# Reordering Pool's work in a mixture-of-experts stage: row adds behind an expert's own loads, earlier gathers, gate products first

## The chip, the cores and the metric

The kernel runs on all 8 NeuronCores of one Trainium2 chip. Each core computes one batch element, and no core talks to another. The metric is the device time of the slowest core, in microseconds (us). Five engines work side by side on a core: TensorE (PE, matrix products), VectorE (DVE), ScalarE (ACT), GpSimd (POOL) and SyncE (SP). They wait for one another through semaphores. Data moves through 16 DMA engines. In this kernel everything that Pool issues (converting weight loads, indirect gathers, indirect adds) goes through one queue, called q0 in the profile; what SP issues goes through q1.

## The reference, cut to what matters

```python
# per batch element: x is (2048, 1024)
x = x + attention(layernorm(x))            # Q = K = V = layernorm(x) @ Wq + bq, one head
n = layernorm(x)
scores = sigmoid(n @ gate_w.T)             # 32 experts
_, ids = top_k(scores + e_bias, 4)         # 4 experts for each token
w = scores[ids] / sum(scores[ids])
g = einsum('th,ehi->tei', n, w1)           # H = 1024, I = 768
u = einsum('th,ehi->tei', n, w3)
a = silu(g) * u * combine                  # combine: w for the 4 chosen experts, 0 else
x = x + einsum('tei,eih->th', a, w2)
```

Each token uses 4 of 32 experts, so a core has 8192 pairs of token and expert, 256 for an expert in the mean. The kernel computes an expert only for the tokens that chose it.

## The kernel before, in words

**First stage.** Attention, the second layer norm and the routing run first. Normalized tokens are written to device memory as bf16 (`xnd`), `out` receives the attention result, and the routing writes for each expert a list of its tokens with their weights. `t_meta` holds these lists: for each expert three blocks of 128 places (`NB = 3`), each place a row number and a weight. Places that no token takes point to spare rows behind the 2048 real ones. `t_cnt` holds the number of tokens for each expert. Weights of the first experts are loaded during this stage.

**Weights.** An expert has three weight units: `w1`, `w3` and `w2`, numbered `3*ei`, `3*ei+1`, `3*ei+2`. A unit is 128 partitions of 6144 values. `load_unit` reads it as f32 from device memory and the DMA converts it to bf16: 768 pieces with 2 KB on the destination side, issued by Pool. 16 of the 96 units (`CONV`: 7 to 10, then 17, 24, ... 94) were converted to device memory during the first stage and come through SP's queue instead. On chip there are 11 places (`RING`), so unit `u` can be loaded once unit `u-11` has been used: the places of expert `ei` receive w2 of expert `ei+3` and then w1 and w3 of expert `ei+4`.

**One expert**, on TensorE in this order:

- `gu(ei)`: for each of 6 column blocks a gate product (w1) and an up product (w3), each 8 matmuls of 128x384, into four PSUM banks of `pss`: banks 0 and 1 for gates, 2 and 3 for ups, by turns. ScalarE takes SiLU of a gate bank into `sil` (two places), VectorE multiplies with the up bank into `at`.
- `tx(ei+1)`: 24 transposes of the gathered rows `xg` of the next expert, copied by ScalarE into `xgt`. It waits for that expert's gather.
- `w2(ei)`: for three blocks and two halves, 6 matmuls of 128x512 into one of two banks of `pav`. VectorE and ScalarE evict them, scaled by the routing weight, into `yb`. `yb` has 6 buffers, which is two experts, so these evictions wait until the row adds of expert `ei-2` have landed (`y_sc.get(ei - 2)`).

`gather(ei)` is three indirect DMAs, 128 rows each, into `xg` (two experts deep; it waits for `tx(ei-2)`). `scatter(ei)` is three indirect DMAs that add rows of `yb` to `out` in device memory; it waits until the adds of expert `ei-1` have landed, because two experts can add to the same row. Blocks 0 and 1 always add 128 rows, the last block 32, 64, 96 or 128, picked by branches on the count.

**Pool's order** is the order of these calls. For one expert it is: load the places of w1 and w3 after all of `gu(ei)`; `scatter(ei-1)`; `gather(ei+2)`; load the place of w2 after `w2(ei)`. Pool works through its list in order, so one instruction that waits holds up all behind it.

## Time and profile before

| what | value |
|---|---|
| median of 3 runs | 1649.07 us (1647.56 to 1649.4) |
| profiled execution, its own time | 1663.17 us |
| span of its slowest core (core 1) | 1661.7 us |
| spans of the 8 cores | 1633.3 to 1661.7 us |
| TensorE, busy share of the span | 75% |
| ScalarE, VectorE, Pool, busy share | 26%, 24%, 24% |
| q0 packets over the whole span, share of 16 DMA engines | 98816, 85.2% |

All views are of core 1 in one profiled execution. "Busy" counts an engine's instructions. Pool's instructions that issue DMAs are spans of issuing, not of the transfer. A DMA queue's share is the time that its packets took, over 16 engines and the stretch; two queues can overlap on an engine, so shares can add up to more than 100%. The first stage ends near 502 us, the expert stage runs from there to the end.

### The profile page before, as it was taken

The numbers are of one execution on the slowest core, as the hardware profiler recorded it, in microseconds if no ns is written. First come the engines' busy times: TensorE is split into PE (matmuls) and PEld (weight loads), VectorE is DVE, ScalarE is ACT, GpSimd is POOL, SyncE is SP. The second block draws the span as 40 slices with busy tenths as digits, with TensorE's granted clock in tenths as the row PEclk, the third lists the DMA queues.
The fourth block names the chain that finished last, engine by engine and source line by source line (L and its number), as shares of the span: only waits on it lengthen the run. The fifth ranks groups of instructions, "written<-read, shape, count | busy, mean of one in ns | idle before, by whom it ended". The sixth has DMA issues, their size and how long they took to land.

```text
span 1661.7 us, 20590 instructions; the slowest of 8 cores (1633.3 to 1661.7 us)
## 1 busy us (share of the span) xinstructions
PE 1248.2 (75%) x7210; PEld 706.6 (43%) x7210; DVE 396.6 (24%) x864; ACT 434.9 (26%) x623; POOL 405.4 (24%) x375
## 2 busy tenths in 40 slices
PE   3989999988736958666969586769696668596696
PEld 1544555554423534333535343434353334353353
DVE  3634444444341211111111111111121111121121
ACT  2743333333212212111312121212121122132131
POOL 0000202112442222232322222323222223232222
PEclk8989989888767979788979798889798798798798
DMA  7999999999642999999999999999999999999933
GB/s 166 219 191 231 239 184 230 212 222 211 140 178 44 167 192 178 189 166 188 168 180 168 190 167 182 173 182 162 188 166 187 182 183 173 187 163 176 175 68 58
DMA packets 112392, 291.80 MB, mean 176 GB/s; under 512 B 11703, under 2 KB 12087, under 8 KB 107936
## 3 DMA queue, kind: packets, MB, share of 16 engines
q0 software_dynamic: 98816, 234.86, 85.2%
q1 hardware_dynamic: 13328, 55.58, 10.5%
q8 instruction: 59, 0.97, 0.2%
q14 instruction: 45, 0.37, 0.1%
q10 hardware_dynamic: 144, 0.03, 0.0%
HBM read 374.37 MB, written 77.63 MB: 272 GB/s over the span
## 4 chain that ended last, share of the span: by engine, by line
PE 40%; DMA 38%; issue 7%; POOL 5%; ACT 4%; DVE 4%; another core or an unknown queue 1%; POOLq 0%; DVEq 0%; ACTq 0%; SPq 0%
DMA xg<-xnd,t_meta 24%; PE pss L834 13%; DMA out<-yb,t_meta 12%; PE pav L865 8%; PE pav L518 7%; PE pss L478 4%; POOL out L889 3%; PE ptr L569 3%; PE ptr L350 3%; PE pss L397 2%; POOL xg L803 1%; DMA wq<-wqd 1%; ACT xn L593 1%; ACT xgt L821 1%
## 5 line engine op out<-in xcount | busy, mean ns | idle before, releaser
L834 PE MATMUL pss<-xgt,wp 128*128 128x384 bf16 x2016 | 338.9, 328 | 1.4 <-ACT xgt L821 1.4
L350 PE MATMUL ptr<-c_idb,xg 128*128 128x128 bf16 x768 | 75.5, 270 | 307.0 <-DMA xg<-xnd,t_meta 288.6
L834 PEld LDWEIGHTS pss<-xgt,wp 128*128 128x128 bf16 x2016 | 197.9, 98 | 135.7 <-issue 4.4
L889 POOL DMA_INDIRECT out<-yb,t_meta x96 | 146.7, 1529 | 279.2 <-DMA out<-yb,t_meta 184.1
L848 DVE TENSOR_TENSOR at<-sil,pss 128x384 bf16<-128x384 bf16 x192 | 106.4, 554 | 449.0 <-PE pss L834 447.0
L350 PEld LDWEIGHTS ptr<-c_idb,xg 128*128 128x128 bf16 x768 | 62.9, 122 | 323.7 <-issue 323.3
L874 DVE TENSOR_SCALAR yb<-pav,t_meta 128x512 f32<-128x512 f32 x96 | 72.0, 750 | 526.2 <-PE pav L865 502.9
L821 ACT COPY xgt<-ptr 128x1024 bf16<-128x1024 bf16 x96 | 97.2, 1012 | 350.9 <-PE ptr L350 321.5
L845 ACT ACTIVATE sil<-pss 128x384 bf16<-128x384 f32 x192 | 94.3, 491 | 358.1 <-PE pss L834 358.1
L834 PE MATMUL pss<-xgt,wr 128*128 128x384 bf16 x1056 | 178.8, 326 | 0.0
L865 PE MATMUL pav<-wp,at 128*128 128x512 bf16 x756 | 178.4, 397 | 0.3 <-DVE yb L874 0.2
L834 PEld LDWEIGHTS pss<-xgt,wr 128*128 128x128 bf16 x1056 | 103.3, 98 | 69.4
L518 PE MATMUL pav<-vq,pt 128*128 128x512 bf16 x512 | 126.5, 410 | 0.0
L478 PE MATMUL pss<-qt 128*128 128x512 bf16 x512 | 120.8, 391 | 0.7 <-ACT c_srep L454 0.4
L865 PEld LDWEIGHTS pav<-wp,at 128*128 128x128 bf16 x756 | 75.2, 102 | 94.8 <-issue 26.6
L877 ACT ACTIVATE yb<-pav,t_meta 128x512 f32<-128x512 f32 x96 | 66.0, 687 | 189.0 <-PE pav L865 185.8
L803 POOL DMA_INDIRECT xg<-xnd,t_meta x96 | 100.1, 1043 | 30.0 <-issue 29.2
L865 PE MATMUL pav<-wr,at 128*128 128x512 bf16 x396 | 95.9, 404 | 1.0 <-DVE at L848 1.0
L518 PEld LDWEIGHTS pav<-vq,pt 128*128 128x128 bf16 x512 | 54.5, 108 | 66.9 <-issue 17.8
L252 POOL DMA_DIRECT2D wp<-w2d x22 | 18.7, 848 | 257.3 <-PE pss L834 189.8
L478 PEld LDWEIGHTS pss<-qt 128*128 128x128 bf16 x512 | 50.7, 100 | 58.0 <-issue 7.6
L569 PE MATMUL ptr<-c_gw,x2t 128*128 128x32 f32 x256 | 49.6, 369 | 33.9 <-ACT x2t L551 33.9
(98 smaller groups left out, 839.1 us busy)
## 6 DMA issues: line engine op xcount, KB each, us to landing
wp<-w3d POOLq DMA_DIRECT2D x26, 1536.0 KB, 26.9
wp<-w1d POOLq DMA_DIRECT2D x23, 1536.0 KB, 30.9
wp<-w2d POOLq DMA_DIRECT2D x22, 1536.0 KB, 31.8
wcd<-wp POOLq DMA_DIRECT2D x16, 1536.0 KB, 24.9
xb<-xd SPq DMA_DIRECT2D x32, 512.0 KB
wr<-w2d POOLq DMA_DIRECT2D x10, 1536.0 KB, 26.0
wr<-w1d POOLq DMA_DIRECT2D x9, 1536.0 KB, 36.1
wr<-wcd SPq DMA_DIRECT2D x8, 1536.0 KB, 13.6
```

The lines of the kernel that those rows point to most:

```text
L350: ins = e.transpose(dst[:, k * 128:(k + 1) * 128], src_of(k), ident)
L478: ins = e.matmul(pss[:, q * 512:(q + 1) * 512], qt[:, c * T + j * 128:c * T + (j + 1) * 128], qt[:, c * T + q * 512:c * T + (q + 1) * 512] ...
L518: ins = e.matmul(pav[:, hh * 512:(hh + 1) * 512], pt[:, (j % 2) * T + c * 128:(j % 2) * T + (c + 1) * 128], vq[:, c * H + hh * 512:c * H + ...
L569: ins = e.matmul(ptr[:, b * 512 + i * E:b * 512 + (i + 1) * E], x2t[:, o:o + 128], c_gw[:, c * E:(c + 1) * E], start=(c == 0), stop=(c == ...
L803: ga_tok[ei] = p.d(lambda e, o=o, c=c: e.indirect_dma_start(out=xg[:, o:o + H], out_offset=None, in_=xnd[:, :], in_offset=bass.IndirectOff ...
L821: tr_tok[k] = txe_tok[ei] = p.s(lambda e, b=b, dst=dst: e.copy(dstv[:, :, b * 128:(b + 1) * 128], dst.rearrange("p (c t) -> p c t", c=NH)) ...
L834: ins = e.matmul(pss[:, bnk * 512:bnk * 512 + CAP], unit_ap(u, c * ID + ic * 128, 128), xgt[:, xo + c * CAP:xo + (c + 1) * CAP], start=(c ...
L845: sl_tok[n] = p.s(lambda e, so=so, gb=gb: e.activation(sil[:, so:so + CAP], pss[:, gb * 512:gb * 512 + CAP], AF.Silu), tg, a_tok.get(n - 2))
L848: a_tok[n] = p.v(lambda e, so=so, ub=ub, ic=ic: e.tensor_tensor(at[:, ao + ic * CAP:ao + (ic + 1) * CAP], sil[:, so:so + CAP], pss[:, ub * ...
L865: ins = e.matmul(pav[:, hh * 512:(hh + 1) * 512], at[:, ao + ic * CAP + b * 128:ao + ic * CAP + (b + 1) * 128], unit_ap(3 * ei + 2, ic * H ...
L874: ybank[0] = p.v(lambda e, dst=dst, src=src, wcol=wcol: e.tensor_scalar(dst, src, wcol, None, ALU.mult), w2_tok[ei], t_ml, y_sc.get(ei - 2))
L889: return e.indirect_dma_start(out=outd[:, :], out_offset=bass.IndirectOffsetOnAxis(ap=t_meta[0:n, 2 * c:2 * c + 1], axis=0), in_=yb[0:n, y ...
```

## The change

Three things change, all in the expert stage.

1. **Order on Pool.** `gather(2)` is issued before the loop. For each expert the order becomes: load the place of w1 (now after the gate products only), load the place of w3 (after the up products), `gather(ei+3)`, load the place of w2, `scatter(ei)`. A gather is issued as soon as `tx(ei+1)` has freed its buffer.
2. **Rows added.** Block 0 still adds 128 rows. Blocks 1 and 2 both pick 16, 32, ... 128 rows by a tree of branches on the count (three compares deep, eight leaves).
3. **Order on TensorE.** `gu` computes all six gate products, then all six up products. `sil` grows from two to six places, and the four banks of `pss` are used by turns over both.

```diff
@@ -166,7 +166,7 @@
         xg = sb("xg", 2 * NB * H, BF16)
         xgt = sb("xgt", 2 * NH * CAP, BF16)
         at = sb("at", 2 * NI * CAP, BF16)
-        sil = sb("sil", 2 * CAP, BF16)
+        sil = sb("sil", NI * CAP, BF16)
         yb = sb("yb", 6 * H, F32)
 
         pss = st.enter_context(nc.psum_tensor("pss", [128, 2048], F32))
@@ -780,6 +780,7 @@
             out=t_meta[:, :].rearrange("q (b n) -> q b n", b=NB), in_=mtv),
             "dML", p.cnt("dSC"), t_mi)
 
+        g_tok = {}
         gu_tok = {}
         w2_tok = {}
         tx_tok = {}
@@ -826,30 +827,34 @@
         def gu(ei):
             xo = (ei % 2) * NH * CAP
             ao = (ei % 2) * NI * CAP
+
+            def mm(e, u, bnk, ic):
+                for c in range(NH):
+                    ins = e.matmul(pss[:, bnk * 512:bnk * 512 + CAP],
+                                   unit_ap(u, c * ID + ic * 128, 128),
+                                   xgt[:, xo + c * CAP:xo + (c + 1) * CAP],
+                                   start=(c == 0), stop=(c == NH - 1))
+                return ins
+
             for ic in range(NI):
-                gb, ub = ic % 2, 2 + ic % 2
-
-                def mm(e, u, bnk, ic=ic):
-                    for c in range(NH):
-                        ins = e.matmul(pss[:, bnk * 512:bnk * 512 + CAP],
-                                       unit_ap(u, c * ID + ic * 128, 128),
-                                       xgt[:, xo + c * CAP:xo + (c + 1) * CAP],
-                                       start=(c == 0), stop=(c == NH - 1))
-                    return ins
-                tg = p.t(lambda e, mm=mm, gb=gb: mm(e, 3 * ei, gb),
+                n = ei * NI + ic
+                gb = ic % 4
+                tg = p.t(lambda e, gb=gb, ic=ic: mm(e, 3 * ei, gb, ic),
                          txe_tok[ei], u_tok[3 * ei], *bank[gb])
-                tu = p.t(lambda e, mm=mm, ub=ub: mm(e, 3 * ei + 1, ub),
+                sl_tok[n] = p.s(lambda e, gb=gb, ic=ic: e.activation(
+                    sil[:, ic * CAP:(ic + 1) * CAP], pss[:, gb * 512:gb * 512 + CAP], AF.Silu),
+                    tg, a_tok.get(n - NI))
+                bank[gb] = (sl_tok[n],)
+            g_tok[ei] = tg
+            for ic in range(NI):
+                n = ei * NI + ic
+                ub = (NI + ic) % 4
+                tu = p.t(lambda e, ub=ub, ic=ic: mm(e, 3 * ei + 1, ub, ic),
                          u_tok[3 * ei + 1], *bank[ub])
-                n = ei * NI + ic
-                so = (n % 2) * CAP
-                sl_tok[n] = p.s(lambda e, so=so, gb=gb: e.activation(
-                    sil[:, so:so + CAP], pss[:, gb * 512:gb * 512 + CAP], AF.Silu),
-                    tg, a_tok.get(n - 2))
-                a_tok[n] = p.v(lambda e, so=so, ub=ub, ic=ic: e.tensor_tensor(
-                    at[:, ao + ic * CAP:ao + (ic + 1) * CAP], sil[:, so:so + CAP],
+                a_tok[n] = p.v(lambda e, ub=ub, ic=ic: e.tensor_tensor(
+                    at[:, ao + ic * CAP:ao + (ic + 1) * CAP], sil[:, ic * CAP:(ic + 1) * CAP],
                     pss[:, ub * 512:ub * 512 + CAP], ALU.mult),
                     tu, sl_tok[n], w2_tok.get(ei - 2))
-                bank[gb] = (sl_tok[n],)
                 bank[ub] = (a_tok[n],)
             gu_tok[ei] = tu
 
@@ -893,26 +898,26 @@
                         in_=yb[0:n, yo:yo + H], in_offset=None,
                         bounds_check=bound(e, TROWS - 1), oob_is_err=True, compute_op=ALU.add)
 
-                def add_last_rows(e, done, b=b, add_rows=add_rows):
-
+                def add_counted_rows(e, done, b=b, add_rows=add_rows):
+
+                    def pick(lo, hi):
+                        if lo == hi:
+                            done(add_rows(e, lo))
+                            return
+                        mid = (lo + hi) // 32 * 16
+                        with e.If_lt(cnt_reg, b * 128 + mid + 1):
+                            pick(lo, mid)
+                        with e.Else():
+                            pick(mid + 16, hi)
                     e.reg_load(cnt_reg, t_cnt[0:1, ei:ei + 1])
-                    with e.If_lt(cnt_reg, b * 128 + 33):
-                        done(add_rows(e, 32))
-                    with e.Else():
-                        with e.If_lt(cnt_reg, b * 128 + 65):
-                            done(add_rows(e, 64))
-                        with e.Else():
-                            with e.If_lt(cnt_reg, b * 128 + 97):
-                                done(add_rows(e, 96))
-                            with e.Else():
-                                done(add_rows(e, 128))
+                    pick(16, 128)
 
                 waits = [*ye_tok[(ei, b)], *prev]
-                if b < NB - 1:
+                if b == 0:
                     y_sc[ei] = p.d(lambda e, add_rows=add_rows: add_rows(e, 128), "dY", *waits,
                                    eng="gpsimd")
                 else:
-                    y_sc[ei] = p.put("gpsimd", add_last_rows, [*waits, v_cnt], "dY", 16,
+                    y_sc[ei] = p.put("gpsimd", add_counted_rows, [*waits, v_cnt], "dY", 16,
                                      branches=True)
 
         gather(0)
@@ -920,22 +925,19 @@
         tx(0)
         for eng in Prog.ENGINES:
             p.put(eng, lambda e: e.reg_load(ovf_reg[e.engine], t_flag[0:1, 0:1]), [v_ovf])
+        gather(2)
         for ei in range(E):
             gu(ei)
             tx(ei + 1)
             w2(ei)
 
             us = [u for u in range(RING, 3 * E) if (u - RING) // 3 == ei]
-            for u in us:
-                if (u - RING) % 3 < 2:
-                    load_unit(u, gu_tok[ei])
-            if ei >= 1:
-                scatter(ei - 1)
-            gather(ei + 2)
-            for u in us:
-                if (u - RING) % 3 == 2:
-                    load_unit(u, w2_tok[ei])
-        scatter(E - 1)
+            for u, tok in zip(us, (g_tok[ei], gu_tok[ei])):
+                load_unit(u, tok)
+            gather(ei + 3)
+            for u in us[2:]:
+                load_unit(u, w2_tok[ei])
+            scatter(ei)
         p.put("gpsimd", None, [p.cnt("dY")])
 
         ovf = nc.alloc_registers("ovf")
```

## Rows read from the trace of the kernel before

**Rows 1.** Cores: span and mean granted TensorE clock of the slowest.
```profile
core 1: 1661.7 us, clock 0.868
```

**Rows 2.** Waits, 515 to 1561 us: waiter <- awaited: us in total, times, longest.
```profile
PE ptr L350 <- DMA xg<-xnd,t_meta: 257.5, 26, 19.9
POOL wp L252 <- PE pss L834: 233.1, 16, 14.9
POOL wr L252 <- PE pss L834: 184.7, 11, 21.1
POOL out L889 <- DMA out<-yb,t_meta: 184.1, 15, 15.8
```

**Rows 3.** Busy time by stretch; last three: granted clock, DMA share, GB/s.
```profile
514.00:526.00 12.00, 11.17 (x54) 6.05 (x55) 1.65 (x3) 3.33 (x5) 0.00 (x0) 0.75 0.00 0
526.00:535.00 9.00, 8.20 (x65) 5.28 (x64) 1.68 (x4) 2.71 (x5) 1.37 (x2) 1.00 0.01 2
535.00:1561.00 1026.00, 737.42 (x4351) 416.97 (x4348) 156.16 (x252) 224.02 (x335) 274.37 (x238) 0.87 1.05 177
1561.00:1662.00 101.00, 85.55 (x504) 47.38 (x504) 18.97 (x30) 26.20 (x39) 28.16 (x21) 0.92 0.43 79
```

**Rows 4.** DMA queues, 535 to 1561 us: packets, MB, share of 16 engines.
```profile
q0 software_dynamic: 72966, 162.25, 99.2%
q1 hardware_dynamic: 1728, 18.88, 5.8%
q8 instruction: 36, 0.59, 0.2%
```

**Rows 5.** DMA, 1053 to 1062 us, only weights and few gather packets.
```profile
q0 software_dynamic: 761, 1.53, 104.5%
```

**Rows 6.** DMA, 1064 to 1069 us, almost only row adds.
```profile
DMA packets 285, 0.97 MB, mean 194 GB/s; under 512 B 34, under 2 KB 34, under 8 KB 285
...
q0 software_dynamic: 285, 0.97, 102.5%
```

**Rows 7.** DMA, 1597 to 1608 us, the row adds of expert 29 alone.
```profile
DMA packets 337, 1.20 MB, mean 109 GB/s; under 512 B 48, under 2 KB 48, under 8 KB 336
...
q0 software_dynamic: 336, 1.18, 63.4%
```

**Rows 8.** DMA, 502 to 514 us, the gathers of experts 0 and 1.
```profile
q0 software_dynamic: 480, 1.15, 34.4%
```

**Rows 9.** Pool in order of time, first experts: start, us, what [idle before].
```profile
533.63 0.89 POOL L252 DMA_DIRECT2D wp<-w2d  x1 [22.67 <-PE ptr L350]
...
535.67 1.07 POOL L803 DMA_INDIRECT xg<-xnd,t_meta  x1 [0.27 <-issue]
...
559.32 0.86 POOL L252 DMA_DIRECT2D wp<-w2d  x1 [14.27 <-PE pss L834]
...
561.27 1.66 POOL L889 DMA_INDIRECT out<-yb,t_meta  x1 [0.27 <-issue]
```

**Rows 10.** Pool in order of time, a middle expert.
```profile
1103.24 0.85 POOL L252 DMA_DIRECT2D wp<-w1d  x1 [14.43 <-PE pss L834]
1117.94 1.67 POOL L889 DMA_INDIRECT out<-yb,t_meta  x1 [13.85 <-DMA out<-yb,t_meta]
```

**Rows 11.** Chain that ended last, 1540 to 1662 us: start, us, what.
```profile
1523.87 37.42 DMA xg<-xnd,t_meta
...
1574.07 15.60 PE pss L834 x96
1589.67 0.46 PE ptr L350 x8
...
1591.97 7.78 PE pav L865 x36
...
1649.97 0.02 issue
...
1651.98 1.33 POOL out L889
```

## The prediction

> **What bounds the kernel now.** I read the cores first: the slowest spans 1661.7 us [rows 1], and every number below is of that core. Then the waits of the expert stage [rows 2]: TensorE's one large named wait is for gathered rows, 257.5 us in 26 waits. That invites "the gathers are late", but lateness in a queue has a cause, so I read the busy time by stretch and the queues. From 535 to 1561 us TensorE is busy 737 of 1026 us, while the DMA share is 1.05 [rows 3], and q0 alone holds 99.2% of all 16 engines [rows 4]. So for these 1026 us q0 never runs dry: a gather is late because it stands behind some 35 us of other packets (37.42 us from issue to landing at 1523.87 [rows 11]). Moving packets inside a full queue does not empty it sooner. What counts is when the queue starts, how much it carries, and how much TensorE work is left when it ends.
>
> The two ends show that. From 514 to 535 us the DMA engines stand idle (share 0.00 and 0.01 [rows 3]) while TensorE already works on expert 0; Pool's first load leaves at 533.63 [rows 9], because it waits for all of gu(0). At the other end the last gather that TensorE waits for, expert 29's, lands at 1523.87 + 37.42 = 1561.3 [rows 11]. From there TensorE has no wait worth naming and 101 us still pass with a DMA share of 0.43 [rows 3]: w2(28), three experts of 25.7 us (gu 15.60; 2.30 from the first transposes at 1589.67 to w2 at 1591.97; w2 7.78), and 11.7 us from the end of the products at 1649.97 to the end of the span.
>
> **The prices in q0**, worked out from q0's own balance. Before 1561 the queue carried units 11 to 93 without the 11 that come through SP, 72 loads of 768 packets. Adds of experts 0 to 26 are in it too. For their size I evaluated the routing on the reference's inputs: batch element 1 gives 8256 rows for these 27 experts (9696 for all 32). A row: expert 29 alone has 128 + 128 + 32 = 288 rows, and 336 packets less 48 small ones are these 288; 63.4% of 11 us is 6.97 us, 24.2 ns for each [rows 7]. In a stretch of almost only adds, 285 - 34 = 251 rows took 5 us x 102.5%, 20.4 ns [rows 6]. I take 22. Gathers: 34.4% of 12 us for two experts, 2 us each [rows 8]. The queue's time is 99.2% of 1026 = 1018 us [rows 3, 4]; less 8256 x 0.022 = 182 and some 54 for 27 gathers, 782 us remain for 72 loads: 10.9 us each. A stretch of almost only weights gives 9.0 x 1.045 x 768/761 = 9.5 us [rows 5], the lower bound; with rows at 20.4 ns and gathers at nothing the balance gives 11.8, the upper one.
>
> The Trainium skill (DMA: Bandwidth & Descriptors, "Anatomy of one DMA — SWDGE (gpsimd) path") prices such a DMA at 2 us plus bytes over 436 GB/s, which for 1.57 MB would be a variable part of 3.6 us; the trace does not agree (9.5 to 10.9 us), and by the page the terms (b) and (c) below would be 7.2 and 6.5 us, the total 23.7 with (a) and (d). The measurement decides.
>
> **The change part by part.**
>
> (a) *Gate products first.* Pool's first load may leave after the gates of expert 0, not after its ups. gu(0) runs from 514.8 to 533.1 at a granted clock of 0.75 in its first 12 us [rows 3]; half of it is over near 525.5. The first load leaves at about 526 instead of 533.63, **-8 us**; bounds -6 and -9. From then on each load arrives before the queue runs out: 10.9 us of work each, against places that come free at 526, 534, 544, 551, 559. Banks and `sil` cost TensorE nothing: a bank is used again after four groups of 1.3 us, its eviction takes 0.5 us.
>
> (b) *Order.* Where does TensorE stand now? w2(ei) follows tx(ei+1), so gather(ei+1). Before, that gather was issued directly behind scatter(ei-2), and both behind the two loads after gu(ei-1). Now gather(ei+1) is issued in iteration ei-2, one expert earlier, and is no longer what ends last. But evictions of w2(ei) still need scatter(ei-2) landed (`y_sc`), and that one is now directly behind the loads of iteration ei-2, ahead of the two loads of iteration ei-1. So the wait moves from the gather to the adds, and the adds stand **two loads earlier in the queue: 2 x 10.9 = -21.8 us** (bounds -19 and -23.6). This is a shift of TensorE's position once, not a gain for each expert; it is cashed at the end.
>
> (c) *Fewer rows.* With steps of 16 for blocks 1 and 2, the counts give 8720 rows instead of 9696. Of the 976 saved, 688 belong to experts 0 to 26, ahead of the point that matters: 688 x 22 ns = **-15.1 us** (-14.0 to -16.6). (d) gather(2) is issued before the queue fills: -2 us.
>
> Scatter(26), which releases w2(28), then lands at 1561.3 - 8 - 21.8 - 15.1 - 2 = 1514.4 (before, w2(28) began after 1561.3).
>
> **The end, walked through.** Behind it stand units 92 and 93 and gather(30): 1514.4 + 21.8 + 2 = 1538.2; then scatter(27), 176 rows, 3.9 us: 1542.1 (unit 94 comes through SP); unit 95 and gather(31): 1555; scatter(28), 240 rows: 1560.3. TensorE: w2(28) to 1521, gu(29) to 1536.6, tx(30) waits for its gather, to 1541.5, w2(29) waits for scatter(27), to 1549; from here nothing is late: gu(30) 1564.6, tx(31) 1567, w2(30) 1574.7, gu(31) 1590.3, VectorE's last multiplication 1, w2(31) 1599.3. The old tail of 11.7 us, plus about 1 us for the third compare: 1612. So of the 46.9 us, all but the small stop at 1541.5 to 1542 reach the end, and two experts fewer follow the last wait: **1661.7 - 1612 = 49.7 us less** in the profiled execution. Its own time is 1663.17; the median is 1649.07, so I put the predicted median at 1649.07 - 49.7, **1600**.
>
> **Waits that are added.** scatter(ei) waits on Pool until scatter(ei-1) has landed, and the loads of iteration ei+1 are queued behind it. It waits so already (184.1 us in 15 waits [rows 2], 13.85 us at 1117.94 [rows 10]). I cost it at nothing, covered by the queue: when scatter(ei-1) lands, q0 still holds three loads and a gather, some 33 us, 24 where one load is SP's. Pool needs 5 us for three adds. The branches cost Pool some 2 us more for an expert; it waits 233 + 185 us for TensorE now [rows 2], and only the last tree is on the path. If that cover is gone, each us beyond it leaves q0 dry and costs one us for each expert.
>
> A rule that speaks against it: the Trainium skill (Runtime: NRT & Kernel Launch, "Instruction fetch mechanics") says that a taken branch whose target lies outside the two pages in the instruction memory must wait for a fetch through DMA. No wait in this trace is shown as such a fetch; it stands in the last rival.
>
> **The rivals.** *Lead not won* (0.12): something keeps scatter(ei) from being issued early, so TensorE stays where it was against the queue. For it: the adds are serial, and a wait that moves often keeps its size. Against it: Pool's waits before adds are ended by landings, not by TensorE. Only (a), (c), (d): -25, 1624. *Rows free* (0.10): the packets of 4 KB are not what fills the queue. For it: the price of a weight packet varies with other traffic ([rows 5] against the balance). Against it: rows 7 show the adds alone at the same price. -35, 1614. *Queue runs dry* (0.10, slower but for 0.03 where the stops are small): both trees stall Pool, at up to the longest wait of rows 2 for a loaded queue, 15.8 us each. Two such stalls with 10 us of issuing make 42 us in front of a cover of 24 to 33, 9 to 18 us dry for an expert; at 9, 31 x 9 = 279 less 50: 1878. It decides for slower once the stalls take over 1.6 us beyond the cover, some 8 to 12 us for each tree. Against it: q8, the instruction queue, moved only 36 packets in 1026 us [rows 4], and the tree before shows no such stop: the next DMA follows 0.27 us behind the last [rows 9].
>
> **How the numbers follow.** Main case 0.68, 1592 to 1613: the least of each term sums to 41 us, the largest to 51, with 5 us either way because one profiled execution stands 14 us over the median and another core may be the slowest then (they spread over 28 us now). The two weaker cases lie at 1614 and 1624. 1588 to 1628 holds all three with a few us at either side; it leaves out the dry queue and what I have not thought of. 0.2% is about what a measurement of this kernel can tell from no change. Faster 0.90, same 0.03, slower 0.07.
>
> **What would show it.** Right: q0 busy from about 527; its share 99% until it ends; TensorE's wait for gathers nearly gone, and VectorE and ScalarE waiting for the adds before `yb` instead; some 976 fewer 4 KB packets; the last wait on a landing near 1542. Wrong: a q0 share under 97% between 535 and 1500 us (dry queue), Pool waits without a releaser ahead of adds (stalled branches), or the last wait near its old place, 101 us before the end (lead not won).

## The result, and the profile after

The changed kernel took 1610.2 us (median of 4 runs, 1602.32 to 1631.26), the kernel before 1649.24 us beside it: a ratio of 0.9743 with a 95% interval of 0.9699 to 0.9787, which is 42 us less, between 35 and 50. Two more measurements of the same pair gave 0.9714 (0.9656 to 0.9771) and 0.9775 (0.9731 to 0.982). The prediction was 1600 us, 49.7 us less. In some executions of every kernel four cores were granted a lower TensorE clock and took longer, as cores 0 to 3 did in the profile of loads_behind_26 below (0.82 to 0.84, cores 4 to 7 0.87 to 0.89); the ratios leave slow executions out. The profiled execution took 1602.32 us. Its slowest core is core 3 (1600.9 us); core 1, which was read before, is 0.8 us shorter, and the rows below are of core 1 again, so that they stand against [rows 1 to 11].

Busy time by stretch of the changed kernel, core 1 (columns as in [rows 3]), and its queues from 526 to 1505 us:

```profile
510.00:522.00 12.00, 12.00 (x58) 6.39 (x57) 0.00 (x0) 4.23 (x7) 3.00 (x4) 0.76 0.17 52
522.00:535.00 13.00, 12.20 (x85) 7.09 (x84) 4.23 (x8) 3.72 (x4) 3.86 (x5) 1.00 0.85 130
535.00:1505.00 970.00, 750.26 (x4361) 414.31 (x4359) 155.31 (x251) 224.57 (x335) 270.24 (x233) 0.89 1.06 180
1505.00:1601.00 96.00, 79.95 (x468) 43.73 (x468) 18.99 (x30) 23.16 (x36) 25.59 (x19) 0.93 0.51 90
```

```profile
q0 software_dynamic: 71034, 156.76, 99.5%
q1 hardware_dynamic: 1728, 18.88, 5.7%
q8 instruction: 37, 0.61, 0.2%
```

From 535 to 1505 us the DMA share is 1.06, against 1.05 before: the queue is as full as it was. What changed is where it begins and ends. TensorE's busy share of the long stretch rose from 72% (737 of 1026 us) to 77% (750 of 970). Over the whole program q0 moved 97824 packets instead of 98816. That is 992 fewer, where the counts gave 976 rows; on core 3 it is 1008, as counted.

Waits of the expert stage, core 1, 515 to 1500 us (columns as in [rows 2]):

```profile
POOL out L894 <- ACT yb L882: 368.9, 13, 32.3
...
DVE yb L879 <- DMA out<-yb,t_meta: 266.9, 20, 21.1
...
ACT yb L882 <- DMA out<-yb,t_meta: 154.0, 16, 13.8
PE pav L870 <- DVE yb L879: 142.0, 19, 13.6
...
POOL out L894 <- DMA out<-yb,t_meta: 51.8, 3, 17.8
PE ptr L350 <- DMA xg<-xnd,t_meta: 46.7, 10, 6.7
```

This is the exchange that the prediction described. TensorE's wait for gathered rows fell from 257.5 us [rows 2] to 46.7. In its place VectorE and ScalarE wait 266.9 and 154.0 us before they may write `yb`, for adds that must land first, and TensorE waits 142.0 us for VectorE's evictions in `w2`. A learner who compared only totals would see one large wait replaced by another and call it no gain. The longest wait shown is Pool's, 368.9 us in 13 waits before adds. The view names ScalarE's eviction of `yb`, because it comes last; what Pool really waits for is the landing of the adds of the expert before, which also lets that eviction start. For instance, the rows of expert 27 are in `yb` at 1464.4, the adds of expert 26 land at 1505.3, and those of expert 27 leave at 1506.1. This is the wait that the prediction costed at nothing, and the queue did stay full across it.

Pool in order of time, core 1 (start, us, what, idle time before it):

```profile
509.23 0.99 POOL L804 DMA_INDIRECT xg<-xnd,t_meta  x1 [2.84 <-PE ptr L350]
...
521.23 0.89 POOL L252 DMA_DIRECT2D wp<-w2d  x1 [8.46 <-PE pss L833]
529.02 0.85 POOL L252 DMA_DIRECT2D wp<-w1d  x1 [6.91 <-PE ptr L350]
531.56 1.07 POOL L804 DMA_INDIRECT xg<-xnd,t_meta  x1 [1.69 <-PE ptr L350]
...
540.27 1.62 POOL L894 DMA_INDIRECT out<-yb,t_meta  x1 [0.28 <-issue]
542.16 1.58 POOL L894 DMA_INDIRECT out<-yb,t_meta  x1 [0.27 <-issue]
544.02 1.43 POOL L894 DMA_INDIRECT out<-yb,t_meta  x1 [0.27 <-issue]
```

The first load leaves at 521.23, 22.3 us after the first gather (498.96); before it was 30.1 us (533.63 in [rows 9], first gather at 503.54). Between the adds stand 0.27 us, branches and all, the same gap as before an indirect DMA in [rows 9]. The chain that ended last, core 1:

```profile
1464.05 41.27 DMA out<-yb,t_meta
...
1505.41 0.76 DVE yb L879
...
1512.95 15.60 PE pss L833 x96
...
1530.86 7.78 PE pav L870 x36
1538.63 15.60 PE pss L833 x96
...
1556.54 7.78 PE pav L870 x36
1564.32 15.62 PE pss L833 x96
...
1580.90 6.66 PE pav L870 x30
1587.56 0.03 issue
```

The last wait on a landing ends at 1505.4, and it is one for adds: those of expert 26, because `w2` of 28, 29, 30 and 31 follow. From there TensorE works through: 94.7 us to the end, against 100.4 in [rows 11]. On the page of core 3 the chain gives 51% of the span to landings of adds; before, the page of core 1 had 24% for gathers and 12% for adds.

**How the runs are compared.** The spans hold something that the change does not touch. Pool's first gather marks the start of the expert stage, and it starts anywhere from 474 to 538 us, by core and execution, in kernels whose first stage is the same. For instance, core 3 of two of the kernels below:

```profile
537.69 1.05 POOL L803 DMA_INDIRECT xg<-xnd,t_meta  x1 [6.41 <-issue]
```

```profile
480.83 1.05 POOL L804 DMA_INDIRECT xg<-xnd,t_meta  x1 [9.02 <-issue]
```

So beside each ratio the table gives the **expert stage**: span less the start of the first gather, worked out for each of 8 cores, and of these the median. The last column is the mean time of a q0 packet from 600 to 1400 us (share x 16 x 800 us over the packets, median of the cores). Kernels of one session were timed side by side; sessions 1 to 3 ran on three different chips. One profile is one execution: three of the changed kernel give 1099.5, 1110.6 and 1117.2, so a single stage figure is good to some 9 us either way, and the order of the figures within one session says more. The kernel before has one profile only, so each comparison with its 1157.5 carries that spread.

| kernel | session | ratio to before | expert stage, us | range of the cores | ns for a q0 packet |
|---|---|---|---|---|---|
| before | 0 | 1 | 1157.5 | 1149 to 1171 | 224.3 |
| changed | 0 | 0.9743 (0.9699 to 0.9787) | 1099.5 | 1094 to 1108 | 219.6 |
| rows_only | 1 | 0.9882 (0.9823 to 0.9941) | 1135.6 | 1126 to 1148 | 221.1 |
| gates_only | 1 | 0.9988 (0.9935 to 1.0042) | 1147.8 | 1139 to 1160 | 223.4 |
| order_only | 1 | 0.9938 (0.9893 to 0.9983) | 1138.7 | 1131 to 1148 | 222.7 |
| after_again | 1 | 0.9714 (0.9656 to 0.9771) | 1110.6 | 1103 to 1120 | 222.6 |
| adds_late | 2 | 0.9803 (0.975 to 0.9857) | 1115.8 | 1110 to 1125 | 219.8 |
| gather_late | 2 | 0.981 (0.9756 to 0.9863) | 1121.2 | 1116 to 1134 | 218.9 |
| rows_128 | 2 | 1.0247 (1.0189 to 1.0304) | 1179.6 | 1154 to 1191 | 229.0 |
| loads_behind_16 | 2 | 0.9622 (0.9577 to 0.9667) | 1080.9 | 1068 to 1101 | 219.3 |
| after_third | 3 | 0.9775 (0.9731 to 0.982) | 1117.2 | 1110 to 1126 | 222.9 |
| adds_late_2 | 3 | 0.9854 (0.9747 to 0.9962) | 1133.9 | 1129 to 1144 | 222.2 |
| loads_behind_26 | 3 | 0.9623 (0.9579 to 0.9667) | 1102.8 | 1093 to 1121 | 222.5 |
| loads_behind_0 | 3 | 0.9729 (0.9635 to 0.9823) | 1110.7 | 1106 to 1118 | 222.2 |

Cores 4 to 7 alone give 1095.5 us in loads_behind_26 and 1115.3 in after_third.

**What the queue had done by then.** The traces record every packet of q0 with its size and time. In the expert stage the 2 KB packets are pieces of weight loads, 768 for a load, and the 4 KB packets belong to adds and gathers. The next table counts those that started between the issue of the first load and the first eviction of `w2(28)`, the step behind the last wait before and after the change. "Uncovered" is the part of that time which the packets, spread over 16 engines, do not fill. All figures are medians of the 8 cores.

| kernel | first gather to first load, us | first gather to `w2(28)`, us | loads started | 4 KB packets | ns for a 2 KB packet | uncovered, us |
|---|---|---|---|---|---|---|
| before | 29.7 | 1063.5 | 72.97 | 11899 | 226.4 | 9.3 |
| rows_only | 29.2 | 1041.4 | 72.95 | 11146 | 223.9 | 11.4 |
| gates_only | 21.7 | 1054.1 | 72.99 | 11925 | 226.8 | 9.6 |
| order_only | 29.2 | 1043.8 | 71.16 | 11681 | 226.4 | 12.8 |
| changed | 21.4 | 1003.8 | 71.13 | 10952 | 222.9 | 9.8 |
| after_again | 21.7 | 1014.3 | 71.23 | 10952 | 226.0 | 9.9 |
| after_third | 21.7 | 1021.6 | 71.19 | 10954 | 226.7 | 10.5 |
| adds_late_2 | 21.6 | 1037.6 | 72.77 | 11054 | 225.9 | 10.2 |
| gather_late | 21.6 | 1026.9 | 72.89 | 11323 | 222.1 | 12.4 |
| rows_128 | 20.9 | 1079.9 | 70.42 | 13789 | 226.5 | 9.2 |
| loads_behind_16 | 21.2 | 975.6 | 67.52 | 10952 | 222.7 | 20.5 |
| loads_behind_0 | 42.7 | 1004.0 | 68.22 | 10642 | 227.8 | 10.2 |

Read the rows before and changed against each other. `w2(28)` comes 59.7 us sooner. Of that, 8.2 us are the earlier start, 20 us are 1.84 loads fewer (at 226.4 ns a packet, 10.9 us a load) and 18 us are 947 fewer 4 KB packets (at 304.6 ns). These 46 us are the change. The other 14 us are packets that took less time in that one execution, 222.9 ns against 226.4 for the 2 KB ones and 301.6 against 304.6 for the 4 KB ones.

### The profile page after: what moved, and what is told of

Its sections match the earlier page's. It is cut to its first block, busy times and chain, and to the rows that moved or that the text cites. A ratio compares the mean times of both kernels' runs of the same rounds, so it can differ in the third digit from the quotient of the medians.

```text
span 1600.9 us, 20879 instructions; the slowest of 8 cores (1572.0 to 1600.9 us)
## 1 busy us (share of the span) xinstructions
PE 1250.7 (78%) x7210; PEld 698.6 (44%) x7210; DVE 397.5 (25%) x864; ACT 434.6 (27%) x623; POOL 404.6 (25%) x375
## 4 chain that ended last, share of the span: by engine, by line
DMA 53%; PE 27%; issue 8%; DVE 4%; ACT 3%; another core or an unknown queue 2%; POOLq 1%; POOL 1%; DVEq 0%; ACTq 0%; SPq 0%
DMA out<-yb,t_meta 51%; PE pav L518 7%; PE pss L833 5%; PE pss L478 4%; PE pav L870 4%; PE ptr L569 3%; PE pss L397 2%; PE ptr L350 1%; DMA wq<-wqd 1%; ACT xn L593 1%; POOLq L912 1%; ACT x2t L551 1%; DVE t_st L300 1%; DVE t_st L301 1%
## 5 line engine op out<-in xcount | busy, mean ns | idle before, releaser
L833 PE MATMUL pss<-xgt,wp 128*128 128x384 bf16 x2016 | 333.3, 327 | 1.4 <-ACT xgt L822 1.4
L894 POOL DMA_INDIRECT out<-yb,t_meta x96 | 142.9, 1488 | 709.0 <-ACT yb L882 359.1
L870 PE MATMUL pav<-wp,at 128*128 128x512 bf16 x756 | 193.4, 417 | 99.0 <-DVE yb L879 99.0
L833 PE MATMUL pss<-xgt,wr 128*128 128x384 bf16 x1056 | 173.9, 326 | 0.0
L870 PE MATMUL pav<-wr,at 128*128 128x512 bf16 x396 | 104.0, 425 | 64.2 <-DVE yb L879 63.3
L350 PE MATMUL ptr<-c_idb,xg 128*128 128x128 bf16 x768 | 65.4, 246 | 80.3 <-DMA xg<-xnd,t_meta 58.6
L478 PE MATMUL pss<-qt 128*128 128x512 bf16 x512 | 117.5, 383 | 1.2 <-issue 0.7
L350 PEld LDWEIGHTS ptr<-c_idb,xg 128*128 128x128 bf16 x768 | 55.7, 111 | 92.0 <-issue 89.1
L870 PEld LDWEIGHTS pav<-wr,at 128*128 128x128 bf16 x396 | 41.2, 107 | 122.7 <-issue 91.1
L700 POOL DMA_INDIRECT mtd<-t_tok,t_addr x64 | 62.8, 982 | 46.7 <-DVE t_c L712 30.3
```

The lines of the kernel that those rows point to most:

```text
L350: ins = e.transpose(dst[:, k * 128:(k + 1) * 128], src_of(k), ident)
L478: ins = e.matmul(pss[:, q * 512:(q + 1) * 512], qt[:, c * T + j * 128:c * T + (j + 1) * 128], qt[:, c * T + q * 512:c * T + (q + 1) * 512] ...
L833: ins = e.matmul(pss[:, bnk * 512:bnk * 512 + CAP], unit_ap(u, c * ID + ic * 128, 128), xgt[:, xo + c * CAP:xo + (c + 1) * CAP], start=(c ...
L870: ins = e.matmul(pav[:, hh * 512:(hh + 1) * 512], at[:, ao + ic * CAP + b * 128:ao + ic * CAP + (b + 1) * 128], unit_ap(3 * ei + 2, ic * H ...
L894: return e.indirect_dma_start(out=outd[:, :], out_offset=bass.IndirectOffsetOnAxis(ap=t_meta[0:n, 2 * c:2 * c + 1], axis=0), in_=yb[0:n, y ...
```

## The experiments

### The three parts, one at a time

**rows_only**: the kernel before with the new choice of rows.

```diff
-                def add_last_rows(e, done, b=b, add_rows=add_rows):
...
+                def add_counted_rows(e, done, b=b, add_rows=add_rows):
...
-                if b < NB - 1:
+                if b == 0:
```

> The kernel before with only the counted adds (blocks 1 and 2 in steps of 16 rows). Theory (q0 is full, a row costs 22 ns of it): 688 rows less ahead of the last gather that TensorE waits for, so 15 us less, ratio 0.991 (0.990 to 0.992). Rival (4 KB packets are not what fills the queue): within 3 us of before. Rival (branches stall Pool): slower, and Pool waits without a releaser ahead of its adds.

Measured: 0.9882, and 21.9 us less of expert stage (1157.5 - 1135.6), where 15 were worked out. The interval reaches from 10 to 29 us, so the rival of free rows falls and the size stays loose. The count of packets gives it more closely: 753 fewer 4 KB packets at 304.6 ns are 14.3 us, and most of the rest is that packets took less time in this execution. A stall at the branches is not seen in the queue: Pool waits named "issue" ahead of adds sum to 64.3 us in 62 on core 3 (530 to 1490 us), the longest 16.8, where the kernel before had 32.0 in 65 on core 1 (515 to 1561 us, the longest 14.4), but q0 never ran dry (99.2% from 600 to 1400 us). That these are waits on landings for which the view finds no releaser is likely and not shown.

**gates_only**: the kernel before with six gates ahead of six ups, and one load behind the gates.

```diff
-                    load_unit(u, gu_tok[ei])
+                    load_unit(u, (g_tok if (u - RING) % 3 == 0 else gu_tok)[ei])
```

> The kernel before with only the gate products first, and the load into the place of w1 behind them. Theory: q0 starts some 8 us earlier and is full from then on, so 8 us less, ratio 0.995. Rival (the gain is in TensorE's order or in banks): TensorE's time for one expert's products changes from 15.6 us, or the load of every expert landing earlier gives a gain beyond 8 us.

Measured: 0.9988, not told apart from 1; the stage is 9.7 us shorter, which one profile can't tell from nothing either. Pool in order of time, core 1, first gather and first loads:

```profile
498.06 1.05 POOL L804 DMA_INDIRECT xg<-xnd,t_meta  x1 [4.38 <-issue]
...
517.56 0.89 POOL L252 DMA_DIRECT2D wp<-w2d  x1 [12.09 <-PE pss L833]
525.35 0.85 POOL L252 DMA_DIRECT2D wp<-w1d  x1 [6.91 <-PE ptr L350]
```

The first load leaves 19.5 us after the first gather, against 30.1 before; in the median of the cores it is 21.7 against 29.7. So the queue does start earlier, by 8 to 11 us. That this is worth 8 us at the end is in keeping with both figures, but shown by neither: the interval of the ratio is 18 us wide.

**order_only**: Pool's new order with old rows and old products.

```diff
+        gather(2)
         for ei in range(E):
             gu(ei)
             tx(ei + 1)
             w2(ei)
...
+            us = [u for u in range(RING, 3 * E) if (u - RING) // 3 == ei]
+            for u, tok in zip(us, (gu_tok[ei], gu_tok[ei])):
+                load_unit(u, tok)
+            gather(ei + 3)
+            for u in us[2:]:
+                load_unit(u, w2_tok[ei])
+            scatter(ei)
```

> The kernel before with only Pool's new order (gather as soon as a buffer is free, adds behind the expert's own loads), old row counts and old product order. Theory: TensorE stands two loads (21.8 us) and one early gather (2 us) further ahead of the queue, cashed once at the end: 24 us less, ratio 0.9855. Rival (the gathers' lateness was the cost for each expert): far more than 24 us. Rival (the wait only moves to the adds): within 3 us of before.

Measured: 0.9938, 3 to 18 us less, and 18.8 us of expert stage. The expected 24 us lie outside the interval of the ratio, so that expectation was missed. The rival of far more than 24 us falls; the rival of nothing falls by the stage and by the count of the queue (71.16 loads ahead of `w2(28)` in place of 72.97, which are 19.7 us), and by the ratio alone only just. Waits, core 3, 530 to 1490 us:

```profile
DVE yb L874 <- DMA out<-yb,t_meta: 282.5, 21, 22.9
...
ACT yb L877 <- DMA out<-yb,t_meta: 197.4, 21, 17.9
PE pav L865 <- DVE yb L874: 191.3, 22, 17.7
...
PE ptr L350 <- DMA xg<-xnd,t_meta: 33.7, 7, 16.8
```

The order alone makes the whole exchange of waits. The other two parts have no hand in it: TensorE still waits 224.2 us for gathers in rows_only and 246.2 us in gates_only (same stretch, slowest core of each).

**after_again**, all three parts, in the same session.

> The changed kernel itself beside its parts. If the parts are independent in the queue, 15 + 8 + 24 = 47 us less, ratio 0.9715; the first measurement gave 0.9743 (0.9699 to 0.9787).

Measured: 0.9714, 46.9 us less of expert stage. The parts sum to 21.9 + 9.7 + 18.8 = 50.4 us of stage, but this sum leans three times on the one profile of the kernel before. By ratios they sum to 0.0192 against 0.0286; with intervals of 0.005 each the two are not at odds, and do not decide either. What can be said to add up is what the queue carries: 753 and 218 fewer 4 KB packets in rows_only and order_only against 947 in after_again, 1.8 fewer loads in order_only against 1.7, and a start 8.0 us earlier in gates_only against 8.0.

### Which of the two moves gives the lead

**adds_late**: the changed kernel with the adds in their old place.

```diff
             for u, tok in zip(us, (g_tok[ei], gu_tok[ei])):
                 load_unit(u, tok)
+            if ei >= 1:
+                scatter(ei - 1)
             gather(ei + 3)
             for u in us[2:]:
                 load_unit(u, w2_tok[ei])
-            scatter(ei)
+        scatter(E - 1)
```

> The changed kernel with the adds back in their old place: scatter(ei-1) behind the loads into the places of w1 and w3 of expert ei, gathers still one expert early. Numbers are the expert stage, from Pool's first gather to the end, median of the cores: 1157 us in the kernel before, 1100 and 1110 in two profiles of the changed kernel. Theory (w2's evictions wait for the adds of expert ei-2, and these stand behind two loads again): the lead of about 20 us is gone, 1120 to 1132, and VectorE still waits for the adds. Rival (the early gather is what helps): 1100 to 1110, as the changed kernel.

**gather_late**: the changed kernel with `gather(ei + 2)` in iteration `ei`.

```diff
-        gather(2)
         for ei in range(E):
...
-            gather(ei + 3)
+            gather(ei + 2)
```

> The changed kernel with gathers one expert later again (gather(ei+2) in iteration ei), adds directly behind the expert's own loads. Theory: w2(ei) follows a gather that stands behind the two loads of iteration ei-1, so the lead is gone here too, 1122 to 1134 us of expert stage, and TensorE's wait is named gather again. Rival (the adds' place alone helps): 1100 to 1110.

Measured: 0.9803 and 0.981, stage 1115.8 and 1121.2. adds_late fell between its two expectations and gather_late just under its own, and the changed kernel had no profile in that session. So adds_late was run again beside it.

> The changed kernel again, as the measure for the three beside it: expert stage between 1099 and 1111 us as in its two profiles; they differ because a packet of q0 took 1.5% longer in one of them.

> Adds in their old place, gathers early, once more, now beside the changed kernel on one chip: the first run gave 1116 us of expert stage, 5 to 16 us over the changed kernel, where two loads of 10.9 us were expected. Theory: with the same price of a packet 16 to 24 us over the changed kernel of this call. If it is under 10, the adds' place is worth less than two loads.

The repeat gives 1133.9 against 1117.2, 16.7 us; its ratio is 0.9854 against 0.9775, with intervals that overlap. The changed kernel itself missed its expectation (1099 to 1111) by 6 us. Waits of gather_late (core 3) and of adds_late_2 (core 7), 530 to 1490 us:

```profile
PE ptr L350 <- DMA xg<-xnd,t_meta: 217.4, 20, 19.1
```

```profile
DVE yb L879 <- DMA out<-yb,t_meta: 281.0, 19, 23.2
...
ACT yb L882 <- DMA out<-yb,t_meta: 220.6, 18, 20.1
PE pav L870 <- DVE yb L879: 219.8, 20, 20.0
```

Without either of the two moves the lead is gone: 72.8 and 72.9 loads have started ahead of `w2(28)`, nearly the 73.0 of the kernel before, where the changed kernel has 71.2. With late gathers TensorE's wait is named gather again (217.4 us). With late adds it is named adds, as in the changed kernel, and is longer (219.8 us in `w2`; other core, other execution). `w2(ei)` needs both, so it starts with the later one. The chain at the end of adds_late_2 shows the same tail behind a later landing:

```profile
1496.70 39.49 DMA out<-yb,t_meta
1536.28 0.76 DVE yb L879
...
1545.20 15.60 PE pss L833 x96
```

The stage moves less than two loads of 10.9 us, and the count says why. Both versions put two loads back ahead of the last wait by Pool's order. But when the adds of expert 26 let `w2(28)` start in the changed kernel, q0 has already begun 1.2 loads of those issued behind them (71.2 against the 70 issued ahead), and in adds_late_2 only 0.8 (72.8 against 72). So adds_late_2 has 1.6 loads more ahead of that point, not 2. A 2 KB packet takes 226 to 227 ns in both, so a load takes 10.9 us of the queue and 1.6 loads take 17 us; `w2(28)` comes 16.0 us later. gather_late costs 21.7 us against the changed kernel of session 0, by a comparison across sessions.

### The price of a row

**rows_128**: the changed kernel adding 128 rows in every block.

```diff
-                if b == 0:
+                if b < NB:
```

> The changed kernel, but all three blocks add 128 rows: 12288 rows in place of 8720, no branches. Theory (22 ns of q0 for a row): 2800 rows more ahead of TensorE's last wait, 62 us, and 5 us from longer adds behind it: expert stage 1162 to 1180 us, against before 1.01 to 1.02. Rival (rows are not what fills q0): below 1125.

Measured: 1.0247, stage 1179.6. Core 1's q0 over the whole program:

```profile
q0 software_dynamic: 101408, 245.47, 87.9%
```

These are 3584 packets more than in the changed kernel (97824), the rows put back. The stage is at the upper end of what was expected, the ratio above it (1.01 to 1.02). The stage is longer by 62 us against the slowest profile of the changed kernel and by 80 against the fastest. Some 4 us of that come behind the last wait. Up to `w2(28)` it is 58 to 76 us for 2800 rows: 21 to 27 ns for a row. From the packets alone, 2837 more of 4 KB and their whole time, it is 23 ns. The rival (under 1125) falls. The mean q0 packet is the longest of all runs, 229.0 ns, with more packets of 4 KB among them, and those at 317 ns.

### Does a place in the queue pay once or for each expert?

From here on the question was whether the account of the mechanism also finds a better order. Three versions issue gather and adds ahead of all three loads of an iteration, from expert 16, 26 or 0 on; up to there they keep the changed kernel's order.

```diff
+            if ei < 16:
...
+            else:
+                gather(ei + 3)
+                scatter(ei)
+                for u, tok in zip(us, (g_tok[ei], gu_tok[ei], w2_tok[ei])):
+                    load_unit(u, tok)
```

> The changed kernel, but from expert 16 on Pool issues gather(ei+3) and scatter(ei) first and the three loads of the iteration behind them. The work in q0 is the same; three loads move from ahead of scatter(26) to behind it. Theory: scatter(26) lands 33 us earlier, gather(30) and scatter(27) are then late by some 12 us, as three loads stand ahead of them: about 17 us less than the changed kernel, expert stage 1083 to 1093 us, and TensorE's last wait on a landing is one expert later. Rival (q0 runs dry, as loads wait behind the adds' landing): q0's share falls under 97% after expert 16 and the time is no better than the changed kernel's.

> Loads behind the adds from expert 26 on only. Theory (TensorE's place against the queue counts once, at the end): the whole gain of the version that switches at expert 16 is there, 15 to 22 us less than the changed kernel of this call. Rival (an order gains something for each expert): under a third of it, less than 6 us.

> Loads behind the adds from expert 0 on: the first load now waits for w2(0) and its adds. Theory (q0 is full from its first load on, so its start counts us for us): the first load leaves some 20 us later than in the changed kernel, and this eats the gain of the order: within 6 us of the changed kernel of this call. Rival (the early start is hidden): 15 to 22 us less than the changed kernel, as when it begins at expert 16.

loads_behind_16 measured 0.9622 and 1080.9 us of stage, 2 us under the expected range and 18.6 less than the changed kernel of session 0, whose packets took as long; the sum had 17. The queue did not stay quite full: from 1050 to 1430 us q0's share is 96.4 to 98.6% by core, under the 97% of the rival on two cores, where the changed kernel has 98.9 to 101.1%. Ahead of `w2(28)` 20.5 us are uncovered, not 9.8. The gain outweighs this loss of some 10 us. Its chain, core 3:

```profile
1442.56 31.18 DMA out<-yb,t_meta
...
1473.84 0.76 DVE yb L879
...
1480.07 15.60 PE pss L833 x96
1495.67 9.56 another core or an unknown queue
...
1505.37 1.02 PE ptr L350 x8
...
1517.87 15.60 PE pss L833 x96
```

Adds (of expert 26) now land at 1473.8, and the stop of 9.6 us in front of transposes at 1505.37 is TensorE's wait for gather(30) (the chain has no releaser for it; the place in the order gives it), which the sum had put at 12. One expert less follows the last wait: 74 us remain.

loads_behind_26 changes the order for six iterations only and measured 0.9623, where the changed kernel of that session had 0.9775: 25 us less by ratio, 14.4 us of stage, 19.8 by the cores 4 to 7 alone in both profiles. So the gain is there within the noise; a gain for each expert would have left under 6 us. What it removes can be read in the changed kernel: on core 1 there, the first eviction of `w2(28)` comes 42.9 us after that of `w2(27)`, where TensorE's own work for an expert is 25.7 us, so the stop costs some 17 us. In loads_behind_26, on core 4, the last wait on a landing ends at 1436.1 and TensorE works through the remaining 148 us without another. loads_behind_0 measured 0.9729 and 1110.7. Pool in order of time, core 1:

```profile
479.65 1.05 POOL L804 DMA_INDIRECT xg<-xnd,t_meta  x1 [8.25 <-issue]
...
516.12 1.61 POOL L894 DMA_INDIRECT out<-yb,t_meta  x1 [0.65 <-DVE yb L879]
...
522.50 1.46 POOL L252 DMA_DIRECT2D wp<-w2d  x1
523.41 1.44 POOL L252 DMA_DIRECT2D wp<-w1d  x1
524.29 1.38 POOL L252 DMA_DIRECT2D wp<-w3d  x1
```

Its first load leaves 42.9 us after the first gather, 20.6 later than in the changed kernel. Against the changed kernel it keeps 6.5 us of stage, at the edge of the 6 that were expected. Against loads_behind_26 it loses 7.9 us of stage, 14.3 by the cores 4 to 7, and 0.0106 by ratio, 17 us, which has an error as large as itself (that of loads_behind_0 rests on two executions). So the late start is not hidden, and costs 8 to 17 us. Less than 20.6 was to be expected: gather(3) and the adds of expert 0 now run ahead of the first load, some 310 packets of 4 KB that the changed kernel carries behind it, an estimated 6 us from the table.

## Why the prediction came out as it did

**The queue is the bound: shown.** A q0 share of 99.5% in the changed kernel from 526 to 1505 us, and all seven profiles with another order on Pool keep the share at 98 to 99.5% from 600 to 1400 us in the median of the cores. What moves the time is what stands ahead of the last wait: more rows, more loads, a later start, each in its direction.

**(a) Earlier start, -8 us: right as to the start.** The first load leaves 8.0 us sooner in gates_only and 8.2 in the changed kernel. Its worth at the end is not told apart from nothing by gates_only alone; that a start counts is shown by the opposite test, loads_behind_0, which loses 8 to 17 us for a start 20.6 us later.

**(b) Order, -21.8 us by two loads: right in kind, a little large.** Only both moves together give it, and it is cashed once, at the end. The price of a load was right: 768 packets of 223 to 227 ns on 16 engines are 10.7 to 10.9 us. The number of loads was the part that came out smaller: 1.84 fewer stand ahead of `w2(28)` in the changed kernel (20 us), 1.81 in order_only, 1.58 between after_third and adds_late_2. The lower bound of 9.5 us from [rows 5] was one fast stretch. Taken over all 3 us slices of all cores that hold nothing but weight packets, a load takes 10.3 to 10.7 us in the kernel before and in the changed kernel of sessions 0 and 3. The mean from the queue's balance is not inflated by what adds do to their neighbours: in the kernel before a 2 KB packet takes 230 ns in such slices and 231 in slices shared with 4 KB packets. In rows_128 it is 224 against 229; a small effect of many adds stays open.

**(c) Rows, -15.1 us: right.** 753 fewer 4 KB packets in rows_only are 14.3 us, and rows_128 gives 21 to 27 ns for a row, 23 from its packets, against 22. The stage of rows_only (21.9 us) and its ratio (10 to 29 us) do not contradict this.

**The sum.** The four terms gave 46.9 us. Counted in the queue they are 46 (8.2 for the start, 20 for loads, 18 for rows and the early gather together). The sum also had 2.8 us less behind the last wait (1612 - 1514.4 = 97.6 against 100.4). This did not come: from the first eviction of `w2(28)` to the end the cores take 94 us before and 96 after. So 44 us are left of the 49.7, close to the 42 of the ratio. The prediction was right for its own reasons, and not by luck. The 58 us by which the stage of the first pair of profiles differs, and the 61.6 us of core 1, would have spoken for a larger effect than there is: 14 of them are shorter packets in that execution.

**The walk through the end.** Adds of expert 26 were put at 1514.4 and landed at 1505.4; the first gather of that execution was 4.6 us early, so the sum was 4 us off. The stops at 1538 to 1542 did not come. `w2(28)` took 7.5 us after its landing, not 6.6, and with gu(29) at 15.6 the transposes came at 1528.55, 23.1 us after the landing, when by the sum the queue should have delivered gather(30) after 23.8. It had done so sooner: the adds of expert 27, which stand behind gather(30), have landed by 1527.9, when Pool stops waiting for them (12.06 us before the adds of expert 28). The sum let both loads begin only when the adds of expert 26 had landed, and q0 had begun 1.2 of them by then. The tail behind the products grew from 11.7 to 12.5 us (1587.56 to 1600.1), the "about 1 us" for the third compare.

**From the profile to the median.** 61.6 us less on core 1 (1661.7 to 1600.1), 42 by the ratio: the two profiled executions lie on opposite sides of their medians, and 4.6 of the 61.6 us are the first stage. The 49.7 us of the prediction are at the upper edge of the ratio's interval (35 to 50). The prediction took 0.2% for what a measurement of this kernel can tell; the intervals here reach 0.4 to 1% either way.

**The signs.** Four of the signs of being right came: q0 busy from 522 us on, its share at 99%, TensorE's wait for gathers at 46.7 us with VectorE and ScalarE waiting for adds instead, and 992 fewer packets. The fifth did not: the last wait on a landing ends at 1505.4, not near 1542, and 94.7 us before the end. That is near the 101 us which the prediction had named as a sign that the lead was not won. The sign was badly chosen. The lead moves the last wait to an earlier time, but the wait stays at the same place in TensorE's order, ahead of `w2(28)`, so the work behind it stays nearly the same.

**The rivals.** *Lead not won*: falls, by adds_late_2 and gather_late, which are what it would look like (72.8 and 72.9 loads ahead of `w2(28)` against 71.2). *Rows free*: falls, by rows_128. *Queue runs dry*: falls for this change (share 99.5%, uncovered time 9.8 us against 9.3); no stop for branches is seen. The cover is not wide: Pool stands up to 32.3 us before adds in the changed kernel, where the prediction counted on 24 to 33 us of work in the queue, and loads_behind_16 loses some 10 us of the queue. The Trainium skill's rule on instruction fetch (Runtime: NRT & Kernel Launch, "Instruction fetch mechanics") describes a stall for a taken branch to a far target; in this case 0.27 us stand between adds with three compares each, and the instruction queue q8 moved 37 packets in the long stretch against 36 in [rows 4]. So no run here shows such a stall.

The versions that beat both kernels are loads_behind_16 and loads_behind_26, at 0.962 of before; which of the two is better is not shown.

## What to carry to other kernels

When a DMA queue is full from start to end, a wait for a transfer says where the waiter stands in the queue, not what the transfer costs: ask what fixes the queue's start, what it carries ahead of the last wait, and how much work follows that wait. Order inside such a queue pays once, at the end, so what releases the longest remaining work should go first and bulk loads whose turn is far off last; but the same order can delay the queue's first transfer, and what the queue then stands idle is lost at the end. If two things gate the same step, moving only one shows nothing. Where two executions differ by more than the change can give, count the packets ahead of the last wait and their mean time: the first is the change, the second the execution.

## What the runs showed of the hardware that was not expected

- The first stage, which no version changes, ended (first gather) between 474 and 538 us. That spread is larger than the whole change. Measuring from a marker inside each core takes it out; what is left is a spread of 1099.5 to 1117.2 us for one kernel.
- The mean time of a q0 packet in the same kernel was 219.6, 222.6 and 222.9 ns in three profiles. By the table this alone moves `w2(28)` by an estimated 12 and 15 us (10.5 and 17.8 us measured).
- A converting load of 1.57 MB took 10.7 to 10.9 us of a full queue, and 10.3 to 10.7 us in slices with nothing else. The Trainium skill (DMA: Bandwidth & Descriptors, "Anatomy of one DMA — SWDGE (gpsimd) path") prices the variable part by bytes over 436 GB/s, an estimate of 3.6 us for the bf16 bytes written and 7.2 us for the f32 bytes read. Both are under what was measured, and the measurement decides.
